# A fused vision-text layer with routed experts: two groups of short products spread among longer ones

## The chip, the cores and the metric

The kernel runs on one core of one Trainium2 chip. The metric is the device time of one execution in microseconds (us). Names used below: PE is TensorE (PEld its weight loads), DVE is VectorE, ACT is ScalarE, POOL is GpSimd, SP is SyncE.

## The reference

Images are cut into patches and embedded, joined with text tokens to 32 sequences of 165 tokens of width 192, and go through a linear attention and a softmax attention. What matters here is the end of the last layer, on all 32 x 165 = 5280 tokens:

```python
x = x + gelu(x @ mlp_w1 + mlp_b1) @ mlp_w2 + mlp_b2      # the plain layer, 192 -> 768 -> 192
xm = _ln(x, ln2_g, ln2_b)
logits = xm @ gate_w.T + gate_b                          # 4 experts
topv, topi = jax.lax.top_k(logits, 2)
gates = jax.nn.softmax(topv, axis=-1)
comb = jnp.einsum('bnk,bnke->bne', gates, onehot)
for e in range(4):
    he = gelu(xm @ exp_w1[e] + exp_b1[e])
    moe_out = moe_out + comb[..., e:e + 1] * (he @ exp_w2[e] + exp_b2[e])
return x + moe_out
```

## The kernel before

The attention part fills the first 770 us and is not touched. The plain layer works on GROUPS = 11 groups of GT = 480 tokens, each group as TG = 4 tiles of TB = 120. On every engine a function `step(n)` holds the work of group n, in an order written out by hand; semaphores alone tie the engines together. After the eleven steps come 25 turns of `turn(i)`, one for each tile of 480 rows of an expert's list, from turn -1, which only has a first layer.

PE's part of step n, in its order:

- `up(n)`: the first layer, KH = 6 blocks of five products with 480 moving columns each (operands split in a high and a low part: XH, XL, XS), alternating between banks 2 and 3. ACT takes each block with a gelu to GF and copies its high part to GH, DVE makes the low part GL.
- `tokens_in(n + 1)`: eight transposes of the next group's tokens X (in step 10 `rows_T(0)`, of expert rows RT).
- `down(n, ..., (0, 1))`: output tiles 0 and 1 of the second layer, into banks 4 and 5. A tile is KH pairs of products, one with GH (384 columns) and one with GL (192), and a bias product. In tile 0 each pair waits until its GL is there.
- `gated_T(n - 1)`: eight transposes of the normed output R of the group before; ACT scales them into ZF.
- output tile 2 (bank 6).
- `gate(n - 1, n)`: the router's logits, four tiles of two fp32 products with only 4 moving columns. The trace shows each fp32 product as two records, so one gate is 16 of them. They go to the end of bank 7.
- `prefix(n - 2, n)`: eight products of the chosen experts `sel` (16, 12, 8 and five times 4 columns), which count how many tokens before each one go to the same expert; to the end of bank 4, for the last two groups of bank 7.
- output tile 3 (bank 7).

DVE's part of step n: `mlp_sum(n - 1)` (X<-PS, twice) and the layer norm's statistics (`st`, `mv`, `ve`) among GL of blocks 0 to 3, then `x2_normed` (R<-X,mv,rs, L1294), which needs POOL's `rs` (L696), then GL of blocks 4 and 5, then the low parts of the next group's tokens (XL, XS), in steps 1 to 4 the low part of an expert's weights (w2r, 1.36 us), in step 8 `plan_early()` (L1354 to L1371), and then the router of group n - 2: `routing` (lg, top, ldf, ..., sel), `weights` (which waits for POOL's `lex`), `prefix_read` and `positions` (pos, carry, ..., dest).

POOL's part of step n: `rs` of group n - 1, the transfer of X to out, two row transfers to the experts' lists (expert_rows<-R,dest), `lex` (which needs `ldf`), two more, and four of the next group, which need `dest`.

Semaphores named by the change: `zf_ready` (ACT has made ZF), `ldiff_ready` (DVE has made ldf, the last reader of the gate's columns in bank 7), `sel_ready`, `down_read` (DVE has read the output banks), `prefix_read_done`. In turn 0 the order on PE is `up` for tile 1 with `gated_T(10)` in its middle, output tiles 0 to 2, `gate(10)`, `rows_T(2)`, `prefix(9)`, output tile 3; in turn 1 `prefix(10)` stands ahead of output tile 3. ACT's `row_high(2)` and DVE's `row_low(2)` (XL<-ZF,XH, L1249) need `rows_T(2)`, and the first layer of tile 2 needs them.

## Time and profile before

| | us |
|---|---|
| median of 3 runs (lowest, highest) | 1386.32 (1385.67, 1396.26) |
| profiled execution | 1383.22 |
| its span, first to last instruction | 1381.5 |
| PE, DVE, ACT, POOL busy in it | 1253.2, 986.9, 664.1, 423.0 |
| mean granted clock of TensorE | 0.961 |

All views below are of the one profiled execution, whose own time is 1383.22 us: 1.7 us lie outside its span. Times in the views count from the start of the span. A granted clock of 1.00 is 2.4 GHz, 0.50 is 1.2 GHz. Steps 0 to 10 begin (first product of `up`) at 771.93, 788.81, 807.08, 828.02, 847.71, 868.10, 888.46, 908.72, 928.82, 949.92 and 970.26 us, turn -1 at 989.97 us.

### The profile page before, as it was taken

What the parts mean: (1) busy time and instruction counts of PE and PEld (TensorE: products, weight loads), DVE (VectorE), ACT (ScalarE), POOL (GpSimd) and SP (SyncE); (2) the same over time, 40 slices, a digit from 0 to 9 for tenths busy, and PEclk for the clock granted to TensorE, in tenths of its full rate; (3) what the DMA queues carried; (4) which work ended last, traced back from release to release, by engine and by line L of the source; (5) the groups of instructions that cost most, each with busy time, mean ns of one, the idle gap of its engine ahead of it and who ended that gap; (6) DMA issues with size and microseconds to landing.
All of it is one profiled execution on the core that took longest, in us unless ns stands there. A gap on an engine that the chain in (4) does not pass through costs nothing.

```text
span 1381.5 us, 28231 instructions
## 1 busy us (share of the span) xinstructions
PE 1253.2 (91%) x9938; PEld 1052.7 (76%) x9938; DVE 986.9 (71%) x2685; ACT 664.1 (48%) x1520; POOL 423.0 (31%) x395
## 2 busy tenths in 40 slices
PE   4589999999999999999987899999989999999996
PEld 3377777777777777777765788898778899899995
DVE  3367777777777777777764767667778878878884
ACT  0154555545555455554555745434543444444541
POOL 1111111111011110111100037677657544544545
PEclk8689999999999999999997999999999999999998
DMA  2092211022110221102400424235466666666653
GB/s 91 21 253 52 61 52 52 15 60 60 52 52 14 60 60 52 54 13 60 97 8 9 191 46 80 62 83 147 86 183 183 151 165 165 146 178 154 148 123 33
DMA packets 93596, 123.32 MB, mean 89 GB/s; under 512 B 9152, under 2 KB 85801, under 8 KB 89554
## 3 DMA queue, kind: packets, MB, share of 16 engines
q1 hardware_dynamic: 69090, 100.75, 24.3%
q0 software_dynamic: 24432, 21.62, 10.5%
q8 instruction: 42, 0.69, 0.2%
q14 instruction: 32, 0.26, 0.1%
HBM read 68.94 MB, written 53.38 MB: 89 GB/s over the span
## 4 chain that ended last, share of the span: by engine, by line
PE 61%; DVE 19%; issue 11%; POOL 5%; ACT 3%; DMA 1%; POOLq 0%; DVEq 0%; SPq 0%; ACTq 0%
PE PS L1486 52%; PE PS L1489 9%; POOL rs L624 2%; DVE st L1010 2%; POOL expert_rows L690 2%; DVE XA L1021 1%; DVE nb L1086 1%; DVE mv L1013 1%; DVE Z L1021 1%; DVE R L1294 1%; DVE GL L1255 1%; ACT GF L925 1%; DVE H L1053 1%; ACT XAT L744 1%; POOL rs L696 1%
## 5 line engine op out<-in xcount | busy, mean ns | idle before, releaser
L1486 PE MATMUL PS<-w2r,GH 128*120 (+1 forms) x864 | 268.3, 369 | 3.1 <-DVE GL L1255 2.4
L925 ACT ACTIVATE GF<-PS,b1c 128x480 f32<-128x480 f32 x216 | 142.1, 658 | 261.0 <-PE PS L1486 248.7
L624 POOL TENSOR_TENSOR rs<-ve,minus_half 128x3 f32<-128x3 f32 (+1 forms) x80 | 58.9, 736 | 625.9 <-DVE ve L1015 625.9
L728 POOL DMA_INDIRECT out<-YO,ids x100 | 173.2, 1732 | 169.0 <-DVE flag L1439 134.3
L1486 PE MATMUL PS<-w2r,GL 128*120 (+1 forms) x864 | 221.4, 256 | 0.0
L766 ACT ACTIVATE PX<-PS,nb 128x165 f32<-128x165 f32 x576 | 176.9, 413 | 66.2 <-DVE nb L1086 57.7
L1486 PE MATMUL PS<-XH,w1r 128*128 128x480 f32 x432 | 172.3, 399 | 10.1 <-ACT GF L925 4.8
L1486 PEld LDWEIGHTS PS<-w2r,GH 128*120 128x120 f32 x864 | 161.5, 187 | 8.5 <-DVE GL L1255 8.1
L1486 PEld LDWEIGHTS PS<-w2r,GL 128*120 128x120 f32 x864 | 164.2, 190 | 0.0
L1489 PE MATMUL PS<-ident,PX 128*128 128x128 f32 x864 | 138.7, 289 | 19.7 <-DVE PT L1091 11.7
L1086 DVE TENSOR_REDUCE nb<-PS 128x6 f32<-128x990 f32 x96 | 113.5, 1184 | 50.8 <-PE PS L1486 50.4
L1489 PEld LDWEIGHTS PS<-ident,PX 128*128 128x128 f32 x864 | 95.7, 144 | 64.0 <-issue 30.0
L744 ACT ACTIVATE PT<-PS 128x384 f32<-128x384 f32 x144 | 72.6, 504 | 121.4 <-PE PS L1489 121.4
L1486 PE MATMUL PS<-XS,w1r 128*128 128x480 f32 x432 | 130.4, 383 | 0.0
L1091 DVE COPY PT<-PS 128x384 f32<-128x384 f32 x144 | 79.7, 554 | 64.2 <-PE PS L1489 63.8
L1486 PEld LDWEIGHTS PS<-XH,w1r 128*128 128x128 f32 x432 | 83.0, 192 | 43.2 <-ACT GF L925 23.0
L1486 PE MATMUL PS<-K,Q 64*128 64x165 f32 (+1 forms) x1536 | 106.3, 314 | 1.6 <-DVE K L1098 1.2
L690 POOL DMA_INDIRECT expert_rows<-R,dest x88 | 93.4, 1062 | 35.7 <-issue 24.8
L1262 DVE TENSOR_TENSOR GL<-GF,GH 128x480 fp32r<-128x480 f32 x150 | 99.3, 662 | 5.2
L1486 PEld LDWEIGHTS PS<-K,Q 64*128 64x128 f32 (+1 forms) x1536 | 80.5, 160 | 19.3 <-issue 12.1
L1486 PEld LDWEIGHTS PS<-XS,w1r 128*128 128x128 f32 x432 | 82.0, 190 | 12.6
L1486 PE MATMUL PS<-XL,w1r 128*128 128x480 f32 x216 | 82.6, 382 | 0.0
(249 smaller groups left out, 2313.1 us busy)
## 6 DMA issues: line engine op xcount, KB each, us to landing
w1r<-expert_w_parts SPq DMA_DIRECT2D x25, 1536.0 KB, 7.2
expert_rows<-empty SPq DMA_DIRECT2D x45, 369.4 KB, 5.9
RT<-expert_rows SPq DMA_DIRECT2D x25, 369.4 KB, 3.9
X<-x_scratch SPq DMA_DIRECT2D x11, 360.0 KB, 4.1
out<-X POOLq DMA_DIRECT2D x11, 360.0 KB, 5.6
XP<-in_patches SPq DMA_DIRECT2D x32, 108.0 KB
H<-in_txt SPq DMA_DIRECT2D x16, 192.0 KB, 3.8
out<-H SPq DMA_DIRECT2D x16, 192.0 KB
```

Source lines behind the costliest of these rows:

```text
L624: nc.gpsimd.tensor_tensor(rs[:, k - 1, 0:n], ve[:, k - 1, 0:n], eps_half[:, 0:n], ALU.pow).then_inc(rstd_ready[k - 1], 1)
L690: nc.gpsimd.indirect_dma_start(listd[:, :], bass.IndirectOffsetOnAxis(ap=dest[:, n % 2, t, k:k + 1], axis=0), R[n % RBUF][:, t, :], None, ...
L728: nc.gpsimd.indirect_dma_start(out[:, :], bass.IndirectOffsetOnAxis(ap=ids[:, i, t:t + 1], axis=0), YO[:, i % 2, t, :], None, bounds_check ...
L744: return nc.scalar.activation(dst, src, ACT.Copy, scale=scale)
L766: last = nc.scalar.activation(PX[:, u % 2, c, to:to + S], PS[:, 2 * (u % 2) + r, c * S:(c + 1) * S], ACT.Exp, bias=nb[:, u, 3 * r + c:3 * ...
L925: nc.scalar.activation(GF[:, m % 3, :], PS[:, 2 + m % 2, 0:GT], ACT.Gelu, bias=bias, scale=1.0).then_inc(gelu_ready, 1)
L1010: last = nc.vector.bn_stats(st[:, k - 1, t, :], src(t))
L1086: nc.vector.tensor_reduce(nb[:, u, :].rearrange("p (a s) -> p a s", a=2), src, AX_X, ALU.min).then_inc(max_ready, 1)
L1091: cp(*probT_views(g)).then_inc(probT_dve_ready, 1)
L1262: tt(GL[at][:, m, :], GF[:, m % 3, :], GH[at][:, m, :].bitcast(F32), ALU.subtract).then_inc(hid_ready, 1)
L1486: return nc.tensor.matmul(o, l, r, start=start, stop=stop)
L1489: return nc.tensor.transpose(o, x, ident[0:rows, 0:rows])
```

## The change

`gate` now makes one tile per call and `prefix` one of its shifts per call, and both are called from inside `up` and `down`. The gate of group n - 2 stands in step n behind blocks 2, 3, 4 and 5 of `up` (before: the gate of group n - 1 in step n, in one piece ahead of output tile 3). The prefix products of group n - 2 stand behind the first four pairs of output tile 3, the last five of them together behind the fourth. Ahead of output tile 3 PE waits for `ldiff_ready` of group n - 2, since the tile's bank holds the gate that DVE reads. Step 10 keeps a gate in one piece (group 9), besides that of group 8 in `up`; step 1 has none. In turn 0 the gate of group 10 goes behind the pairs of output tile 0, `rows_T(2)` behind tile 0, and the prefix of group 9 among the pairs of tile 2; in turn 1 the prefix of group 10 among those of tile 2. The products themselves and their number stay.

```diff
-        def up(s, at, w, ms):
+        def up(s, at, w, ms, gate_of=None):
...
                 mm(o, w(3, m), xs, False, True).then_inc(up_ps, 1)
+                if gate_of is not None and m >= KH - TG:
+                    gate(gate_of, s, m - KH + TG)
...
-        def down(s, gh, gl, w, bias, ts):
+        def down(s, gh, gl, w, bias, ts, prefix_of=None, gate_of=None):
...
                     mm(bank[:, 0:D], gl[:, k, TB * t:TB * t + TB], w(k, D), False, False)
+                    if prefix_of is not None and k < TG:
+                        prefix(prefix_of, s, k)
+                    if gate_of is not None and k < TG:
+                        gate(gate_of, s, k)
...
-        def gate(n, s):
-
-            pe.wait_ge(zf_ready, n + 1)
-            pe.wait_ge(down_read, s * TG + 3 + 1)
-            if n > 0:
-                pe.wait_ge(ldiff_ready, n)
-            for t in range(TG):
-                o = PS[0:TB, 7, GATE_AT + NE * t:GATE_AT + NE * t + NE]
-                for k in range(2):
-                    last = mm(o, ZF[:, k, TB * t:TB * t + TB], gwf[:, k, :], k == 0, k == 1)
-            last.then_inc(gate_ps, 1)
+        def gate(n, s, t):
+            if t == 0:
+                pe.wait_ge(zf_ready, n + 1)
+                pe.wait_ge(down_read, s * TG + 3 + 1)
+                if n > 0:
+                    pe.wait_ge(ldiff_ready, n)
+            o = PS[0:TB, 7, GATE_AT + NE * t:GATE_AT + NE * t + NE]
+            for k in range(2):
+                last = mm(o, ZF[:, k, TB * t:TB * t + TB], gwf[:, k, :], k == 0, k == 1)
+            if t == TG - 1:
+                last.then_inc(gate_ps, 1)
...
         def step(n, at):
             later = n > 0
             pe.wait_ge(actT_ready, n + 1)
-            up(n, at, mlp_w1, range(KH))
+            up(n, at, mlp_w1, range(KH), n - 2 if n > 1 else None)
...
             down(n, GH[0], GL[0], mlp_w2, b2r[:, 0, :], (2,))
-            if later:
-                gate(n - 1, n)
             if n > 1:
-                prefix(n - 2, n)
-            down(n, GH[0], GL[0], mlp_w2, b2r[:, 0, :], (3,))
+                pe.wait_ge(ldiff_ready, n - 1)
+            if n == GROUPS - 1:
+                for t in range(TG):
+                    gate(n - 1, n, t)
+            down(n, GH[0], GL[0], mlp_w2, b2r[:, 0, :], (3,), n - 2 if n > 1 else None)
...
-                down(GROUPS + i, GH[at], GL[at], w2, b2, (0, 1, 2))
-                if i == 0:
-                    gate(last, GROUPS)
+                    down(GROUPS, GH[at], GL[at], w2, b2, (0,), None, last)
                     rows_T(2)
-                if i < 2:
-                    prefix(last - 1 + i, GROUPS + i)
+                    down(GROUPS, GH[at], GL[at], w2, b2, (1,))
+                else:
+                    down(GROUPS + i, GH[at], GL[at], w2, b2, (0, 1))
                 if i == 1:
                     pe.wait_ge(ldiff_ready, GROUPS)
+                down(GROUPS + i, GH[at], GL[at], w2, b2, (2,), last - 1 + i if i < 2 else None)
```

How this moves the instructions on PE. Before, between output tiles 2 and 3 of each of the steps 2 to 10 (w2r,GH and w2r,GL are a pair of an output tile, b2r,ones its bias product, gwf,ZF the gate, sel the prefix; here a product counts once, not as two records):

```order
L1486 MATMUL PS<-b2r,ones 120x192
L1486 MATMUL PS<-gwf,ZF 120x4 [waits ldiff_ready,down_read,zf_ready]
L1486 MATMUL PS<-gwf,ZF 120x4 x7
L1486 MATMUL PS<-sel,earlier 120x16 [waits prefix_read_done,down_read,sel_ready]
L1486 MATMUL PS<-sel,ones 120x12
L1486 MATMUL PS<-sel,ones 120x8
L1486 MATMUL PS<-sel,ones 120x4 x5
L1486 MATMUL PS<-w2r,GH 120x384 [waits down_read]
```

Now, in the same place:

```order
L1486 MATMUL PS<-b2r,ones 120x192
L1486 MATMUL PS<-w2r,GH 120x384 [waits down_read,ldiff_ready]
L1486 MATMUL PS<-w2r,GL 120x192
L1486 MATMUL PS<-sel,earlier 120x16 [waits prefix_read_done,down_read,sel_ready]
L1486 MATMUL PS<-w2r,GH 120x384
L1486 MATMUL PS<-w2r,GL 120x192
L1486 MATMUL PS<-sel,ones 120x12
```

Two more pairs follow, with the 8-column product behind the first of them and the five of 4 columns behind the second. The gate has gone from here, and the wait for sel stands one pair into tile 3 instead of one gate ahead of it.

Now, on PE at the end of `up` in steps 2 to 10 (XH, XL and XS with w1r are the five products of a block, ident,X the transposes of the next group):

```order
L1486 MATMUL PS<-XS,w1r 128x480 x2
L1486 MATMUL PS<-gwf,ZF 120x4 x2
L1486 MATMUL PS<-XH,w1r 128x480 [waits gelu_ready]
L1486 MATMUL PS<-XL,w1r 128x480
L1486 MATMUL PS<-XH,w1r 128x480
L1486 MATMUL PS<-XS,w1r 128x480 x2
L1486 MATMUL PS<-gwf,ZF 120x4 x2
L1489 MATMUL PS<-ident,X 128x120 [waits x_in0]
```

Each of the last four blocks is followed by one tile of the gate; before, the blocks and the transposes followed each other directly.

## Rows read from the trace of the kernel before

**Rows 1.** The page's parts 1 and 4: busy time, chain that ended last

```profile
PE 1253.2 (91%) x9938; PEld 1052.7 (76%) x9938; DVE 986.9 (71%) x2685; ACT 664.1 (48%) x1520; POOL 423.0 (31%) x395
...
PE 61%; DVE 19%; issue 11%; POOL 5%; ACT 3%; DMA 1%; POOLq 0%; DVEq 0%; SPq 0%; ACTq 0%
```

**Rows 2.** Windows (length, PE busy, PEclk, DMA), gate to next step, ten steps

```profile
803.61:807.08 3.47, 3.47 (x32) 1.00 0.16 37
821.79:828.02 6.23, 6.23 (x39) 0.67 0.08 18
843.41:847.71 4.30, 4.30 (x39) 1.00 0.32 86
...
903.07:908.72 5.65, 5.65 (x39) 0.74 0.27 72
...
985.66:989.97 4.31, 4.31 (x40) 1.00 0.37 99
sum 52.53, PE 52.53; mean PE 5.25
```

**Rows 3.** Windows, the seven stretches at the lower clock

```profile
823.86:830.69 6.83, 6.83 (x26) 0.50 0.10 28
...
sum 27.35, PE 27.35; mean PE 3.91
```

**Rows 4.** Windows, a run of short products in turn 0

```profile
1014.24:1017.48 3.24, 3.24 (x35) 1.00 0.71 214
```

**Rows 5.** Timeline of PE in step 7 (start, length, operation, count)

```profile
923.34 1.76 PE L1486 MATMUL PS<-gwf,ZF 128*120 128x4 f32 x16
...
925.07 0.87 PE L1486 MATMUL PS<-sel,ones 120*120 120x12 f32 x7
...
927.06 0.56 PE L1486 MATMUL PS<-w2r,GH 128*120 128x384 f32 x1
```

**Rows 6.** Timeline of PEld in step 7; brackets: idle time, who ended it

```profile
913.35 0.19 PEld L1486 LDWEIGHTS PS<-XH,w1r 128*128 128x128 f32 x1 [0.25 <-ACT GF L925]
...
917.93 0.18 PEld L1486 LDWEIGHTS PS<-w2r,GH 128*120 128x120 f32 x1 [0.34 <-DVE GL L1255]
```

**Rows 7.** Windows of output tile 0, steps 2 to 10: their sum

```profile
sum 22.39, PE 20.04; mean PE 2.23
```

**Rows 8.** Windows of output tile 2 in step 6

```profile
901.22:902.96 1.74, 1.74 (x15) 1.00 0.34 65
```

**Rows 9.** Timeline of DVE in step 5

```profile
875.10 1.51 DVE L1294 TENSOR_SCALAR R<-X,mv,rs 120x192 f32<-120x192 f32 x4
...
879.49 0.17 DVE L1304 TENSOR_TENSOR ldf<-lg,top 120x16 f32<-120x16 f32 x1
```

**Rows 10.** Timeline of POOL around step 5

```profile
873.68 1.38 POOL L696 TENSOR_TENSOR rs<-ve,minus_half 120x4 f32<-120x4 f32 x1 [2.08 <-DVE ve L1286]
...
879.75 2.98 POOL L683 TENSOR_TENSOR lex<-euler,ldf 120x16 f32<-120x16 f32 x1 [0.18 <-DVE ldf L1304]
...
888.39 1.00 POOL L690 DMA_INDIRECT expert_rows<-R,dest  x1 [0.30 <-issue]
```

**Rows 11.** Timeline of DVE in step 8

```profile
940.12 0.17 DVE L1354 TENSOR_TENSOR jump<-carry,region 120x4 f32<-120x4 f32 x1
...
943.78 0.17 DVE L1304 TENSOR_TENSOR ldf<-lg,top 120x16 f32<-120x16 f32 x1
...
945.03 0.18 DVE L1313 TENSOR_SCALAR sel<-rank 120x16 fp32r<-120x16 f32 x1
```

**Rows 12.** Timeline of DVE in turns 0 and 1

```profile
1019.61 0.66 DVE L1249 TENSOR_TENSOR XL<-ZF,XH 128x480 fp32r<-128x480 f32 x1 [5.90 <-ACT XS L904]
...
1026.64 0.40 DVE L1261 CAST GH<-GF 128x480 fp32r<-128x480 f32 x1
```

**Rows 13.** Timeline of PE in turns 0 and 1

```profile
1021.04 0.45 PE L1486 MATMUL PS<-XH,w1r 128*128 128x480 f32 x1 [1.55 <-issue]
...
1028.64 0.48 PE L1486 MATMUL PS<-XH,w1r 128*128 128x480 f32 x1 [1.85 <-ACT GF L925]
```

More of the change, by code:

```diff
@@ L1829, in prefix @@
-        def prefix(n, s):
-            pe.wait_ge(sel_ready, n + 1)
-            pe.wait_ge(down_read, s * TG + 3 + 1)
-            if n > 0:
-                pe.wait_ge(prefix_read_done, n)
-            o, w = PS[0:TB, prefix_bank(n), PREFIX_AT:PREFIX_AT + TG * NE], TG * NE
-            mm(o, earlier[:, :], sel[:, :], True, False)
-            for d in range(1, TG):
-                mm(o[:, NE * d:w], ones[0:TB, :], sel[:, 0:w - NE * d], False, d == TG - 1)
-            o = PS[0:TB, prefix_bank(n), PREFIX_AT + w:PREFIX_AT + w + NE]
-            for t in range(TG):
-                last = mm(o, ones[0:TB, :], sel[:, NE * t:NE * t + NE], t == 0, t == TG - 1)
-            last.then_inc(prefix_ps, 1)
+        def gate(n, s, t):
[9 more added lines that the diff above has]
+                last.then_inc(gate_ps, 1)
@@ new lines, in prefix @@
+        def prefix(n, s, d):
+            o, w = PS[0:TB, prefix_bank(n), PREFIX_AT:PREFIX_AT + TG * NE], TG * NE
+            if d == 0:
+                pe.wait_ge(sel_ready, n + 1)
+                pe.wait_ge(down_read, s * TG + 3 + 1)
+                if n > 0:
+                    pe.wait_ge(prefix_read_done, n)
+                mm(o, earlier[:, :], sel[:, :], True, False)
+            else:
+                mm(o[:, NE * d:w], ones[0:TB, :], sel[:, 0:w - NE * d], False, d == TG - 1)
+            if d == TG - 1:
+                o = PS[0:TB, prefix_bank(n), PREFIX_AT + w:PREFIX_AT + w + NE]
+                for t in range(TG):
+                    last = mm(o, ones[0:TB, :], sel[:, NE * t:NE * t + NE], t == 0, t == TG - 1)
+                last.then_inc(prefix_ps, 1)
@@ L1868, in step @@
             down(n, GH[0], GL[0], mlp_w2, b2r[:, 0, :], (2,))
-            if later:
-                gate(n - 1, n)
             if n > 1:
-                prefix(n - 2, n)
-            down(n, GH[0], GL[0], mlp_w2, b2r[:, 0, :], (3,))
+                pe.wait_ge(ldiff_ready, n - 1)
+            if n == GROUPS - 1:
+                for t in range(TG):
+                    gate(n - 1, n, t)
+            down(n, GH[0], GL[0], mlp_w2, b2r[:, 0, :], (3,), n - 2 if n > 1 else None)
         tokens_in(0)
```

1 line of the change is left out of this document (added).

## The prediction

> **What bounds the kernel now.** I read the busy times and the chain of work that ended last first: PE is busy for 91% of the span and holds 61% of the chain [rows 1]. The change touches the eleven steps of the plain layer and two turns, about 789 to 1039 us, so the question is what PE's time there is made of. Windows over the ten steps, each from the first gate product to the first product of the next step, answer it. Steps 3 and 10 need 4.30 and 4.31 us for gate, prefix and output tile 3 with the clock granted in full. Seven others hold the same work and need 5.48 to 6.23 us at a mean granted clock of 0.67 to 0.77 [rows 2]. The clock goes to 0.50, the 1.2 GHz level, behind gate and prefix, in seven of the nine steps that have both, and stays there for 3.4 us, in step 2 for 6.8 us; 27.35 us in all [rows 3]. In step 7 the gate's 16 records take 1.76 us and seven prefix products 0.87 us, and the GH products behind them take 0.56 us each [rows 5]; at the full clock they take 0.35 us. PE was never idle there: before each fall it did 2.5 us of products with 4 to 16 columns. Gate alone (step 1) brought no fall [rows 2], nor did gate, transposes and prefix in turn 0 [rows 4].
>
> The second loss of PE in a step is waiting. In output tile 0 it waits for GL of blocks 4 and 5 (0.34 us in one row), in `up` for the gelu of two blocks before (0.25 us in one row) [rows 6]. Nine output tiles 0 take 22.39 us [rows 7], one without waits 1.74 us [rows 8]: 22.39 - 9 x 1.74 = 6.7 us. In `up`, three gaps as in rows 6 occur per step, and part of each hides behind the product before; I take 0.2 us a step, 2.1 us over nine with rounding up: 8.8 us of waits together.
>
> **Direct cost: none.** The number of products stays. A load for a short product takes about 0.105 us of PE's time (2.52 us for 24 of them in step 7, of which rows 5 show the gate's 16 with 1.76). Behind a 480-column product the first load is hidden, but then that of the next block is not, so four records cost four loads again, 0.42 us. Step 1 loses its gate (-1.66 us), step 10 has two (+1.66 us). If spreading cost or saved one load per place, it would be 0.1 us x 8 places x 9 steps = 7 us either way; I take zero, since the loads in rows 5 run at the same rate at both ends of the run.
>
> **The clock: -12.8 us.** Gate to next step in steps 2 to 10 takes 52.53 - 3.47 = 49.06 us; nine times 4.31 are 38.8, so 10.3 us are lost there [rows 2]. The stretches reach 5.0 us in all into the next steps (2.67 of them in step 3: 830.69 - 828.02), at half speed another 2.5 us. With gates between blocks of 1.09 us and prefix products between pairs of 0.28 us, the longest run of short products is five, 0.5 us, where there were 24 in 2.5 us. I expect no fall in steps 2 to 9. Bounds: nothing (the falls stay) and 27.35 / 2 = 13.7 us.
>
> **The waits: -6.6 us.** A gate tile of 0.42 us behind blocks 2 to 5 lets ACT, whose gelu and copy take 1.19 us a block against 1.09 us for PE, catch up; and 0.42 us more PE work lies between block 5 and the pairs that wait for it. DVE pays a little: x2_normed (1.51 us) stands ahead of GL 4 and 5, starting 7.0 us into step 5 and ldf 11.4 us [rows 9]. Behind the stretched blocks GL 5 ends about 0.45 us later, while PE comes to its pair about 0.9 us later. So the 8.8 us would go, but the next limit is near. DVE and POOL form a loop: x2_normed to the end of ldf 4.6 us (875.10 to 879.66), lex 3.15, six row transfers at 1.30 us each 8.0, rs 1.4 [rows 9, 10]: 17.2 us, and 18.5 where DVE makes w2r (1.36 us). PE's own work in a step is 6.54 + 1.66 + 0.75 + 4 x 1.76 + 0.75 + 0.85 = 17.6 us, against 20.1 to 20.4 us for most steps now. I leave 0.4 us each in steps 4 and 5, 0.8 in step 9 (it follows step 8, whose transfers start late) and 0.1 in the others: 2.2 us stay, 6.6 go. Bounds: 8.8 and 0.
>
> **The new waits: +1.2 us.** Ahead of output tile 3 PE now waits for ldf, and one pair later for sel; behind them in PE's queue stand tile 3 and the whole next first layer. In an ordinary step ldf is ready 11.5 us and sel 13.2 us after the start, and PE comes there after about 15.1: nothing. In step 8 plan_early (940.12 to 943.4) comes first, ldf ends 15.1 us after the step's start at 928.82 and sel 16.4 [rows 11]; both shift by 0.5. PE would wait 0.5 us for ldf and 0.9 for sel; of it 0.3 is there already, before the gate, for the same ldf. 1.2 us net; bounds 0.5 and 2.5.
>
> **Step 10: +0.5 us.** It keeps 16 gate records in a row, with a thinned prefix behind them, so a fall (about 1.5 us) stays possible; one in four. The wait ahead of gated_T in this step, for DVE's row_low, stays.
>
> **Turns 0 and 1: -2.7 us.** The first layer of tile 2 starts at 1021.04 after a gap of 1.55 us [rows 13], exactly when DVE has finished XL and XS, which began at 1019.61 after 5.90 us of waiting for ACT [rows 12], which waited for rows_T(2). Moved behind output tile 0, these transposes come 4 us earlier: the 1.7 us go. Block 5 of tile 2 then starts at 1028.64 [rows 13] because the GH that frees its buffer is made at 1026.64 [rows 12], behind row_out, weights, positions and routing of DVE. row_out of tile 3 would begin about 1.7 us earlier in step with PE, and no longer behind row_low and row_out of tile 2; that shortens 2.0 us of wait by 1.0. Bounds: 0 and 3.7.
>
> **Sum.** -12.8 - 6.6 + 1.2 + 0.5 - 2.7 = -20.4 us. Against the profiled execution: 1383.2 - 20.4 = 1362.8. The median before, 1386.3, lies 3.1 us above it, so **1366 us** is the forecast for a median. All bounds at their good ends give 1360, but not all at once; main case 1360 to 1372.
>
> **Rivals.**
>
> - *The freed time turns into waits on DVE and POOL (1374 us).* If the loop above closes at 18.6 us in all nine steps instead of 17.8, because transfers on POOL take 1.4 us now and then and rs comes late, 7 to 8 us come back. For: the loop is only 0.4 us under PE's work. Against: POOL still idles 2.08 us ahead of rs in step 5 [rows 10].
> - *The falls have another cause and stay (1378 us).* Only the waits and the turns count: -6.6 + 1.2 - 2.7 = -8. For: two steps with the same run had no fall. Against: all seven falls come behind this very run, none in a window without it between 777 and 1040 us. The Trainium skill's page "TensorE: Matmul & The Clock Gate", Part 1, ties a fall to stretches in which the PE idles; by that rule a packed run of short products would not count, and moving them would change nothing of the clock. The trace disagrees: PE has no idle time in these windows (5.65 busy of 5.65 us). The same page, Part 4, says that transposes do not count as PE work like products do; by it the last gate tile and the eight transposes now form one stretch. Turn 0, with gate, transposes and prefix in a row and the clock at 1.00, shows that such a stretch alone does no harm.
> - *Slower (1396 us).* If a mixture of short and long products counts as little work, `up` with its gates and transposes and tile 3 with its prefix would each bring a fall: up to 19 of them in place of 7 that cost as much as 8, each 12.8 / 8 = 1.6 us: +17.6, less 8 from waits and turns: +10. It turns slower from 13 falls on. Against: tiles and blocks around make up over half of any such stretch.
> - *Nothing moves (1385 us).* If PE's queue took loads ahead so that the spread makes no difference, and gains end in waits. The order on PE shows the move, so this is small.
>
> **Chances.** Main case 0.62, loop 0.20, falls stay 0.09, slower 0.04, nothing 0.05. A measurement of this kernel tells about 1% (14 us) from no change. Faster by over 1% means below 1372.5: nearly all of the main case and half of the loop case, 0.71. Slower by over 1%: 0.03. The rest, 0.26, lies within. Range: the main case reaches from 1360 to 1372; with the loop case and a part of the third it goes to 1377, and 1359 below leaves room for the median of before.
>
> **What the changed profile would show.** Granted clock 1.00 from 789 to 985 us; steps 5 to 7 at 17.7 to 18.1 us; loads of GH in output tile 0 without gaps; in step 8 a gap at w2r,GH for ldf and one at sel; step 10 about 0.7 us longer than now; the first layer of tile 2 straight behind tile 3. It is wrong if the clock still falls in the steps, or if PE's gaps name GL with rs and R late ahead of it.

## The result and the profile after

In one sitting on one chip the kernel before ran at 1387.04 us (median, 1385.67 to 1396.26) and the changed kernel at 1374.62 us (median of 4 runs, 1368.88 to 1377.07). The ratio is 0.986, 95% interval 0.9823 to 0.9897: faster by 1.4%. The quotient of those two medians is 0.991 and lies outside this interval; the record gives the ratio without its working. Two more sittings with the same kernel gave 0.9869 (0.9835 to 0.9902) and 0.9855 (0.9821 to 0.9889), and there the medians agree with them (0.9855 and 0.9852). One execution of b1 below was slow at 2957.35 us: its ratio leaves it out, its median does not. The profiled execution took 1368.88 us with a span of 1367.1, against 1383.22 and 1381.5.

The page of the changed kernel, parts 1, 2 (TensorE's granted clock) and 4, answers to [rows 1]:

```profile
PE 1236.9 (90%) x9938; PEld 1043.0 (76%) x9938; DVE 986.1 (72%) x2685; ACT 666.7 (49%) x1520; POOL 411.9 (30%) x395
...
PEclk7699999999999999999997899999999999999998
...
PE 59%; DVE 16%; issue 12%; POOL 7%; ACT 3%; another core or an unknown queue 1%; DMA 1%; POOLq 0%; DVEq 0%; SPq 0%; ACTq 0%
```

PE does the same 9938 products in 16.3 us less busy time. The shares of the chain hardly move, but for an entry that stands for updates whose sender the trace does not show; more of that below.

**Where the time went.** I measure each step from the start of its first layer to the start of the next one's, since gate and prefix no longer stand together. Windows of the changed kernel (length, busy time of PE, PEld, DVE, ACT and POOL, then granted clock, DMA share, GB/s): steps 1, 2, 6, 7, 8, 9 and 10:

```profile
787.46:804.05 16.59, 16.02 (x100) 14.14 (x99) 11.52 (x27) 9.36 (x17) 2.83 (x2) 1.00 0.40 98
804.05:821.85 17.80, 17.80 (x125) 16.89 (x123) 14.40 (x45) 9.70 (x16) 5.67 (x3) 1.00 0.28 42
...
876.99:894.78 17.79, 17.79 (x125) 16.87 (x123) 13.42 (x46) 9.69 (x16) 14.22 (x12) 1.00 0.43 85
894.78:912.60 17.82, 17.82 (x125) 16.91 (x123) 13.49 (x46) 9.57 (x16) 13.94 (x12) 1.00 0.42 85
912.60:931.76 19.16, 18.27 (x125) 16.95 (x123) 15.52 (x59) 9.68 (x16) 12.54 (x11) 1.00 0.30 55
931.76:950.71 18.95, 18.36 (x125) 16.84 (x123) 13.88 (x50) 9.56 (x16) 15.86 (x13) 1.00 0.81 230
950.71:971.07 20.36, 19.64 (x141) 18.59 (x139) 13.80 (x49) 11.21 (x18) 14.24 (x12) 1.00 0.50 114
```

All stand at clock 1.00. Steps 3, 4 and 5 take 18.36, 18.31 and 18.47 us. Steps 2 to 9 together, in one window of the kernel before and one of the changed kernel:

```profile
807.08:970.26 163.18, 160.86 (x978) 145.32 (x977) 112.96 (x380) 74.88 (x128) 106.90 (x82) 0.92 0.40 88
```

```profile
804.05:950.71 146.66, 144.91 (x979) 135.16 (x977) 113.32 (x379) 77.02 (x128) 105.67 (x80) 1.00 0.43 93
```

That is 16.5 us less for the same products. Step 1 loses 1.7 us (18.27 to 16.59), step 10 gains 0.65 (19.71 to 20.36), turns -1 and 0 lose 1.7 (31.07 to 29.39), turn 1 gains 0.5 (17.59 to 18.12). Tile 3's turn is 0.05 longer. From the start of step 1 to the start of tile 4's first layer (the "stretch" below) the length falls from 264.67 to 246.02 us: **-18.65 us**. Another 1.35 us were already there at the start of step 1, ahead of everything the change touches. From tile 5 on nothing differs (311.91 and 311.97 us to the end of the span).

**Waits of the steps.** Loads of PE in the changed kernel with the idle time ahead of them: output tile 0 of step 4, output tile 3 of step 8, output tile 0 of step 9:

```profile
850.49 0.18 PEld L1486 LDWEIGHTS PS<-w2r,GH 128*120 128x120 f32 x1 [0.25 <-DVE GL L1255]
851.06 0.18 PEld L1486 LDWEIGHTS PS<-w2r,GH 128*120 128x120 f32 x1 [0.29 <-DVE GL L1255]
...
928.08 0.18 PEld L1486 LDWEIGHTS PS<-w2r,GH 128*120 128x120 f32 x1 [0.34 <-DVE ldf L1304]
...
929.33 0.18 PEld L1486 LDWEIGHTS PS<-sel,earlier 120*120 120x120 f32 x1 [0.97 <-DVE sel L1313]
...
942.67 0.18 PEld L1486 LDWEIGHTS PS<-w2r,GH 128*120 128x120 f32 x1 [0.79 <-DVE GL L1255]
```

The gaps in `up` that [rows 6] show are gone in steps 2 to 9, and with them those of output tile 0 in steps 2, 6, 7 and 8. The two new gaps of step 8 come from DVE's timeline, where the early plan still stands ahead of the routing, as in [rows 11]:

```profile
924.20 0.16 DVE L1354 TENSOR_TENSOR jump<-carry,region 120x4 f32<-120x4 f32 x1
...
927.85 0.17 DVE L1304 TENSOR_TENSOR ldf<-lg,top 120x16 f32<-120x16 f32 x1
...
929.10 0.18 DVE L1313 TENSOR_SCALAR sel<-rank 120x16 fp32r<-120x16 f32 x1
```

**The turns.** Tile 2's first layer now starts at 1000.46, straight behind the last product of tile 3 (1000.35), where [rows 13] have a gap of 1.55 us. Loads of PE in turn 1, and DVE ahead of the second gap:

```profile
1006.98 0.19 PEld L1486 LDWEIGHTS PS<-XH,w1r 128*128 128x128 f32 x1 [1.22 <-ACT GF L925]
1018.54 0.19 PEld L1486 LDWEIGHTS PS<-XH,w1r 128*128 128x128 f32 x1 [1.56 <-issue]
```

```profile
1016.19 0.42 DVE L1436 TENSOR_SCALAR YO<-PS,cs 120x192 f32<-120x192 f32 x1 [3.02 <-PE PS L1486]
...
1017.82 0.65 DVE L1250 TENSOR_TENSOR XS<-ZF,XS 64x480 fp32r<-64x480 f32 x1
```

The gap of 1.56 us is new: tile 3's first layer waits for XS (ends 1018.47), which DVE makes behind `row_out` of output tiles 0 and 1. DVE stood idle for 3.02 us in front of the second `row_out`, although PE's last product of output tile 1 was long issued:

```profile
1012.46 0.26 PE L1486 MATMUL PS<-b2r,ones 128*120 x1
```

The signal of that tile is recorded only at 1016.16, 3.4 us behind the modelled end of this product; in an undisturbed trace such a signal follows within 0.02 us. So the gap doesn't come from the order of DVE's work. It is the first effect of a disturbance that costs more in tile 4's turn.

**A wait that no part of the change explains.** Tile 4's turn takes 21.70 us instead of 16.08. A load of PE, ACT's gelu and DVE's `row_out` there:

```profile
1041.42 0.29 PEld L1486 LDWEIGHTS PS<-XH,w1r 128*128 128x128 f32 x1 [5.99 <-ACT GF L925]
```

```profile
1040.70 0.66 ACT L925 ACTIVATE GF<-PS,b1c 128x480 f32<-128x480 f32 x1 [11.47 <-remote]
```

```profile
1037.74 0.42 DVE L1436 TENSOR_SCALAR YO<-PS,cs 120x192 f32<-120x192 f32 x1 [3.88 <-remote]
```

By the profile, PE's products that ACT and DVE wait for ended long before: the first two blocks ran from 1033.48 to 1035.84, tile 3's last product started at 1033.37. The signals are recorded at 1037.71 for DVE and 1040.57 for ACT, 4.1 and 5.8 us behind. The ends of PE's products are modelled, so the trace can't tell whether the signals or the products themselves were late; "late signal" below means either. PE then stood idle, and the only lower-clock stretch behind step 0 and before the end of the span follows:

```profile
1040.93:1044.34 3.41, 2.92 (x7) 2.48 (x8) 2.96 (x10) 1.51 (x3) 3.10 (x2) 0.50 0.56 56
```

So against the profiled execution of before: -1.35 - 18.65 + 5.6 = -14.4 us. The experiments have two questions: which part of the -18.65 comes from what, and whose are the 5.6 us.

A comparison of the kept traces helps with the second. Of PE's 1154 signals, 21 to 39 come over 0.3 us late or have no record in the changed kernel's trace and in a1 to a4 and c1 to c3; in before, b1 to b4 and d1 it is none or one. Each of the steps 2 to 9 of the changed kernel is within 0.3 us of the same step in b1, so it costs little there. In turn 1 all eight disturbed traces have DVE waits for PE of 1.3 to 3.0 us and the six others have none, b2 with its prefix spread in the same way included.

### The profile page after: what moved, and what is told of

It reads as the page before. It is cut to its first block, busy times and chain, and to the rows that moved or that the text cites. A ratio compares the mean times of both kernels' runs of the same rounds, so it can differ in the third digit from the quotient of the medians.

```text
span 1367.1 us, 28240 instructions
## 1 busy us (share of the span) xinstructions
PE 1236.9 (90%) x9938; PEld 1043.0 (76%) x9938; DVE 986.1 (72%) x2685; ACT 666.7 (49%) x1520; POOL 411.9 (30%) x395
## 4 chain that ended last, share of the span: by engine, by line
PE 59%; DVE 16%; issue 12%; POOL 7%; ACT 3%; another core or an unknown queue 1%; DMA 1%; POOLq 0%; DVEq 0%; SPq 0%; ACTq 0%
PE PS L1486 51%; PE PS L1489 8%; POOL expert_rows L690 3%; POOL rs L624 2%; DVE st L1010 2%; DVE XA L1021 1%; DVE nb L1086 1%; DVE mv L1013 1%; DVE Z L1021 1%; DVE H L1053 1%; ACT XAT L744 1%; POOL out L678 1%; DVE ZS L1068 1%; DVE H L1050 1%
## 5 line engine op out<-in xcount | busy, mean ns | idle before, releaser
L1486 PE MATMUL PS<-w2r,GH 128*120 (+1 forms) x864 | 262.8, 362 | 1.7 <-DVE GL L1255 1.1
L728 POOL DMA_INDIRECT out<-YO,ids x100 | 163.0, 1630 | 184.2 <-DVE flag L1439 158.1
L1486 PE MATMUL PS<-w2r,GL 128*120 (+1 forms) x864 | 216.9, 251 | 0.0
L1486 PEld LDWEIGHTS PS<-w2r,GH 128*120 128x120 f32 x864 | 156.9, 182 | 4.9 <-DVE GL L1255 4.2
L1486 PEld LDWEIGHTS PS<-w2r,GL 128*120 128x120 f32 x864 | 159.1, 184 | 0.0
```

The costliest lines, as they stand in the source:

```text
L728: nc.gpsimd.indirect_dma_start(out[:, :], bass.IndirectOffsetOnAxis(ap=ids[:, i, t:t + 1], axis=0), YO[:, i % 2, t, :], None, bounds_check ...
L1486: return nc.tensor.matmul(o, l, r, start=start, stop=stop)
```

## The experiments

Each kernel was timed in several runs beside the kernel before on the same chip. There were four sittings, each on another chip: a1 to a4, b1 to b4, c1 to c3, d1. The stretch is that of the profiled execution. In the diffs - and + are against the changed kernel, unless another is named.

| kernel | median us | before us | ratio (95%) | steps 1 to 10 | stretch | tile 4's turn |
|---|---|---|---|---|---|---|
| before | | | | 201.16 | 264.67 | 16.08 |
| a1_again | 1368.47 | 1388.60 | 0.9869 (0.9835, 0.9902) | 183.74 | 246.37 | 22.08 |
| a2_gates_spread_only | 1376.72 | 1388.60 | 0.9901 (0.9872, 0.9929) | 187.17 | 249.90 | 22.28 |
| a3_prefix_spread_only | 1388.37 | 1388.60 | 1.0005 (0.9978, 1.0032) | 195.73 | 258.06 | 21.85 |
| a4_turns_only | 1390.64 | 1388.60 | 1.000 (0.9974, 1.0026) | 200.37 | 262.67 | 22.87 |
| b1_steps_only | 1367.25 | 1380.57 | 0.9892 (0.9862, 0.9922) | 183.27 | 246.60 | 15.72 |
| b2_rows_back | 1365.19 | 1380.57 | 0.9892 (0.9862, 0.9922) | 183.41 | 247.77 | 16.08 |
| b3_plan_later | 1369.75 | 1380.57 | 0.9924 (0.9896, 0.9953) | 181.07 | 244.57 | 16.07 |
| b4_gate_behind_up | 1370.30 | 1380.57 | 0.9906 (0.9880, 0.9932) | 185.40 | 249.57 | 16.06 |
| c1_scatter_held | 1370.85 | 1393.56 | 0.9847 (0.9816, 0.9878) | 183.68 | 245.98 | 20.48 |
| c2_load_held | 1376.32 | 1393.56 | 0.9888 (0.9854, 0.9921) | 183.70 | 250.33 | 22.78 |
| c3_as_changed | 1372.91 | 1393.56 | 0.9855 (0.9821, 0.9889) | 183.67 | 246.34 | 21.58 |
| d1_rows_behind_tile1 | 1366.41 | 1387.67 | 0.9847 (0.9812, 0.9883) | 181.67 | 244.17 | 15.72 |

### The changed kernel again, and its parts alone

**a1_again** is the changed kernel unchanged.

> The changed kernel itself once more. Its first profile shows the steps and turns 0 and 1 some 18.6 us shorter than before, as forecast, but then one gap of 6 us (PE waiting for ACT in the first layer of tile 4, with DVE and ACT idle behind late PE signals), which gives 5.6 us back; and its unprofiled runs (1373 to 1377 us) lie above the profiled one (1368.9). Theory A: the gap belongs to the new order (the turns now meet the POOL transfers at another time), then this profile shows it again at the same place, 5 to 6 us. Theory B: it is an accident of that execution, then it is absent or elsewhere and the profiled time is about 1363 us plus or minus 3. Either way the ratio to before should be 0.983 to 0.990.

The wait of tile 4 came again (5.28 us at 1039.86), so it is no accident of one execution.

**a2_gates_spread_only**: gates behind the blocks, prefix in one piece ahead of output tile 3.

```
             if n > 1:
+                for d in range(TG):
+                    prefix(n - 2, n, d)
-            down(n, GH[0], GL[0], mlp_w2, b2r[:, 0, :], (3,), n - 2 if n > 1 else None)
+            down(n, GH[0], GL[0], mlp_w2, b2r[:, 0, :], (3,))
```

> As the changed kernel, but in steps 2 to 10 the eight prefix products stand in one piece ahead of output tile 3 (turns as in the changed kernel). If the clock falls because of the run of 24 short products, then 8 in a row (0.85 us) bring no fall and the time is that of the changed kernel within 2 us. If every short run in that place is enough, falls come back in up to 9 steps and cost 1.6 us each, up to +14 us. The wait for sel in step 8 grows by 0.3 us.

Windows of steps 7 and 8, and the lower-clock stretch in step 8:

```profile
898.23:916.06 17.83, 17.83 (x124) 16.92 (x123) 13.47 (x45) 9.69 (x16) 14.30 (x12) 1.00 0.42 85
916.06:938.40 22.34, 20.40 (x124) 19.24 (x123) 15.72 (x62) 9.44 (x16) 14.78 (x13) 0.89 0.27 53
933.60:940.40 6.80, 6.80 (x26) 6.49 (x27) 3.03 (x11) 0.00 (x0) 5.66 (x5) 0.50 0.15 42
```

An ordinary step is as long as in the changed kernel (17.83 against 17.82): spreading the prefix saves nothing there. Step 8 takes 3.2 us more: PE waits 1.87 us in one piece for sel, up to 933.46, and the clock falls at 933.60, as the packed prefix begins. Here the wait is what stands ahead of the fall; in steps 6 and 7 the same packed prefix without a wait brought none.

**a3_prefix_spread_only**: prefix between the pairs, gate (of the group one later) in one piece ahead of output tile 3.

```
-            up(n, at, mlp_w1, range(KH), n - 2 if n > 1 else None)
+            up(n, at, mlp_w1, range(KH))
...
-            if n > 1:
-                pe.wait_ge(ldiff_ready, n - 1)
-            if n == GROUPS - 1:
+            if later:
                 for t in range(TG):
                     gate(n - 1, n, t)
```

> As the changed kernel, but in the steps the gate of group n - 1 stands in one piece ahead of output tile 3, as before; the prefix stays among the pairs (turns as in the changed kernel). No work now fills PE's waits in up and in output tile 0: by the forecast's terms 6.6 us come back, and no wait for ldf in step 8 beyond that of before (-0.9). The clock: 16 short products and then a thinned prefix; if only the whole packed run makes it fall, it stays at 1.00 (changed kernel +6 us, 1380); if gate and thinned prefix are enough in some steps, +1.5 us for each, up to +13 more.

**a4_turns_only**: the steps in the order of before, turns 0 and 1 as changed.

```
-            up(n, at, mlp_w1, range(KH), n - 2 if n > 1 else None)
+            up(n, at, mlp_w1, range(KH))
...
-            if n > 1:
-                pe.wait_ge(ldiff_ready, n - 1)
-            if n == GROUPS - 1:
+            if later:
                 for t in range(TG):
                     gate(n - 1, n, t)
-            down(n, GH[0], GL[0], mlp_w2, b2r[:, 0, :], (3,), n - 2 if n > 1 else None)
+            if n > 1:
+                for d in range(TG):
+                    prefix(n - 2, n, d)
+            down(n, GH[0], GL[0], mlp_w2, b2r[:, 0, :], (3,))
```

> The steps as before (gate and prefix in one piece ahead of output tile 3), only turns 0 and 1 as in the changed kernel. The forecast's term: 2.7 us faster than before (1384), with the 1.7 us gap ahead of the first layer of tile 2 gone and the seven falls kept. If the new order of the turns is what brings the 6 us gap in tile 4, the profile shows that gap here too and the time is 3 us above before.

Here step 7 can be taken apart. Its window in a4 (gate and prefix in one run, clock falls), and in a3 (gate in one run, prefix spread, no fall in this step):

```profile
910.61:931.01 20.40, 20.10 (x125) 18.19 (x123) 13.30 (x45) 9.34 (x16) 14.26 (x12) 0.92 0.36 74
```

```profile
907.06:926.24 19.18, 18.54 (x124) 16.66 (x123) 13.33 (x46) 9.33 (x16) 14.02 (x11) 1.00 0.40 79
```

In this step a fall costs 1.2 us, not 1.6: the slower PE waits less. The gaps ahead of its loads, added up from the timeline, are 1.42 us in a4 and 1.76 in a3; the difference lies in output tile 0 (0.50 against 0.84). The a3 timeline of PEld shows what stays at the full clock, five gaps; these are the first three and the largest:

```profile
910.27 0.19 PEld L1486 LDWEIGHTS PS<-XH,w1r 128*128 128x128 f32 x1 [0.16 <-ACT GF L925]
911.46 0.19 PEld L1486 LDWEIGHTS PS<-XH,w1r 128*128 128x128 f32 x1 [0.24 <-ACT GF L925]
912.64 0.19 PEld L1486 LDWEIGHTS PS<-XH,w1r 128*128 128x128 f32 x1 [0.24 <-ACT GF L925]
916.52 0.18 PEld L1486 LDWEIGHTS PS<-w2r,GH 128*120 128x120 f32 x1 [0.84 <-DVE GL L1255]
```

With only the prefix thinned out the clock still fell twice in ten steps (886.38 for 3.4 us, 944.41 for 6.8) instead of seven times. So 16 gate records with a thin prefix behind them are sometimes enough.

The timed runs don't agree with the trace of a3: its stretch is 6.6 us shorter than that of before, its ratio 1.0005 (0.9978 to 1.0032), and 1380 us had been expected, or 1383 with its two falls, against a median of 1388. Where the difference went is open. The turns alone measure as nothing: 1.000.

### Apart, but not spread

**b1_steps_only** takes the changed steps with turns 0 and 1 in the order of before.

```
-                    down(GROUPS, GH[at], GL[at], w2, b2, (0,), None, last)
-                    rows_T(2)
-                    down(GROUPS, GH[at], GL[at], w2, b2, (1,))
-                else:
-                    down(GROUPS + i, GH[at], GL[at], w2, b2, (0, 1))
+                down(GROUPS + i, GH[at], GL[at], w2, b2, (0, 1, 2))
+                if i == 0:
+                    for t in range(TG):
+                        gate(last, GROUPS, t)
+                    rows_T(2)
+                if i < 2:
+                    for d in range(TG):
+                        prefix(last - 1 + i, GROUPS + i, d)
...
-                down(GROUPS + i, GH[at], GL[at], w2, b2, (2,), last - 1 + i if i < 2 else None)
```

> The eleven steps as in the changed kernel, turns 0 and 1 in the order of before (gate of group 10 in one piece behind three output tiles, then the row transposes, then the prefix; in turn 1 the prefix ahead of output tile 3). Theory A (the new order of the turns makes the stretch of late semaphore updates and the 6 us wait ahead of tile 4's output): steps at 17.8 to 18.4 us, tile 4 back at about 16 us, median 1362 to 1365, ratio 0.982. Theory B (the stretch comes because everything stands some 18 us earlier against the transfers, whatever the order of the turns): tile 4 takes about 22 us again, median 1369 to 1371.

**b2_rows_back** is the changed kernel with only `rows_T(2)` back behind output tile 2.

```
                     down(GROUPS, GH[at], GL[at], w2, b2, (0,), None, last)
-                    rows_T(2)
...
                 down(GROUPS + i, GH[at], GL[at], w2, b2, (2,), last - 1 + i if i < 2 else None)
+                if i == 0:
+                    rows_T(2)
```

> The changed kernel with one group of row transposes of turn 0 (tile 2's) back behind output tile 2; gate tiles and prefix spread as in the changed kernel. If the early row transposes, which start the load and scatter of later tiles sooner, make the stall of tile 4: tile 4 back at about 16 us, the first layer of tile 2 again 1.5 us late, median about 1364. If the gate products in output tile 0 and the earlier routing make it: tile 4 stays at 22 us, median 1370.

In turn 0 of b1 gate, row transposes and prefix stand in one run again, as in before. There [rows 4] the clock stayed; here it fell 0.3 us behind the run:

```profile
997.96:1001.20 3.24, 3.24 (x35) 3.24 (x33) 0.00 (x0) 0.57 (x1) 2.71 (x2) 1.00 0.68 203
1001.49:1004.90 3.41, 3.22 (x14) 3.00 (x13) 1.49 (x4) 1.81 (x3) 0.00 (x0) 0.50 0.25 27
```

The same run brought a fall in b3 (996.25) and b4 (1009.06, 6.8 us), and PE had no gap in the 8 us ahead of any of the three. One execution in which a packed run kept the clock does not show it harmless.

Windows of tile 4's turn in b1 and in b2:

```profile
1037.09:1052.81 15.72, 14.87 (x92) 13.29 (x91) 14.23 (x46) 6.63 (x10) 11.76 (x9) 1.00 0.70 184
```

```profile
1034.11:1050.19 16.08, 14.88 (x93) 13.29 (x91) 15.02 (x46) 6.52 (x10) 11.52 (x9) 1.00 0.72 186
```

Without the early row transposes tile 4 is back at 16 us in both, and the traces alone would have closed the case: `rows_T(2)` makes the stall. The timings do not agree, and b1's median of 1367 us missed the 1362 to 1365 expected. By the traces b1 should lie 5 us below the changed kernel against the same before, by its ratio it lies level or above (0.9892 against 0.9855 to 0.9869). These two were on another chip than the a kernels; see "Whose are the 5.6 us".

**b3_plan_later** is b1 with DVE's early plan behind the routing.

```
-            if n - 3 == EARLY_GROUPS - 1:
-                plan_early()
             if n > 1:
                 routing(n - 2)
+            if n - 3 == EARLY_GROUPS - 1:
+                plan_early()
+            if n > 1:
                 weights(n - 2)
```

> As the steps-only kernel, and in step 8 DVE makes the early plan behind the routing instead of ahead of it. The waits of step 8 for ldf and sel (0.34 and 0.97 us in the changed kernel) should go and step 8 come to 18.0 us: 1.2 us less than the steps-only kernel, if the 3.3 us of the plan do not come late for the weights; in that case step 9 gets longer by up to 1 us and the sum stays.

Windows of its steps 7 and 8:

```profile
894.47:912.29 17.82, 17.82 (x125) 16.92 (x123) 13.45 (x46) 9.70 (x16) 14.04 (x12) 1.00 0.42 85
912.29:930.07 17.78, 17.78 (x125) 16.87 (x123) 15.85 (x62) 9.69 (x16) 14.05 (x12) 1.00 0.34 65
```

Step 8 loses both waits (19.17 to 17.78) and step 9, whose gap of 0.79 us was its echo, falls from 18.96 to 18.00: 2.35 us for a move of one line. The timed runs did not show it (0.9924 against 0.9892 for b1, overlapping intervals); five of the six ran at a mean clock of 0.962 to 0.966 and the profiled one at 0.972.

**b4_gate_behind_up** is b1 with nothing spread: the gate's 16 records in one piece behind `up`, the prefix in one piece ahead of output tile 3.

```
-            up(n, at, mlp_w1, range(KH), n - 2 if n > 1 else None)
+            up(n, at, mlp_w1, range(KH))
+            if n > 1:
+                for t in range(TG):
+                    gate(n - 2, n, t)
...
+            if n > 1:
+                for d in range(TG):
+                    prefix(n - 2, n, d)
-            down(n, GH[0], GL[0], mlp_w2, b2r[:, 0, :], (3,), n - 2 if n > 1 else None)
+            down(n, GH[0], GL[0], mlp_w2, b2r[:, 0, :], (3,))
```

> As the steps-only kernel, but the gate's 16 records stand in one piece behind the first layer and the prefix in one piece ahead of output tile 3: nothing is spread, the two are only apart. If the fall of the clock needs gate and prefix in one run (24 short products), none comes and the steps take 18.0 to 18.8 us (only the waits inside the first layer, 0.2 us a step, stay): 1 to 4 us above the steps-only kernel. If every packed run of 16 short products brings one, seven to nine falls come back at 1.6 us each: 11 to 15 us above it.

Window of its step 7:

```profile
902.51:920.53 18.02, 18.02 (x124) 16.66 (x123) 13.45 (x45) 9.45 (x16) 14.29 (x12) 1.00 0.41 84
```

This is the experiment that says most of the mechanism. No fall in steps 2 to 9, and they take 147.35 us against 146.37 in b1. (Step 10, which keeps a gate directly ahead of the prefix, had one.) So two runs, of 16 and of 8 short products, three output tiles apart, kept the clock in all eight steps, where one run of 24 lost it in seven of nine. The moved gate also fills the waits of output tile 0 in b4, but missing waits are not what keeps the clock: the packed runs in turn 0 of b1, b3 and b4 had none ahead of them and the clock fell.

The fine spread is worth 1.0 us over eight steps. PE's timeline from the start of `up` to the first transpose of the next group in step 7 shows what it does, in b4 and in the changed kernel:

```profile
902.51 0.41 PE L1486 MATMUL PS<-XH,w1r 128*128 128x480 f32 x1
...
909.30 1.74 PE L1486 MATMUL PS<-gwf,ZF 128*120 128x4 f32 x16
910.91 1.02 PE L1489 MATMUL PS<-ident,X 120*128 120x120 f32 x8
```

```profile
894.78 0.40 PE L1486 MATMUL PS<-XH,w1r 128*128 128x480 f32 x1
...
902.96 1.02 PE L1489 MATMUL PS<-ident,X 120*128 120x120 f32 x8
```

Six blocks without a wait take 6 x 1.09 = 6.54 us. b4 needs 6.79 us for them and 1.61 for the packed gate, 8.40 in all; the changed kernel 8.18 for both. So the waits in `up` cost b4 0.25 us, and the gate costs 1.6 us packed or spread, 0.4 for four records. The three gaps ahead of the loads in b4's `up` (0.16, 0.23, 0.23 us) add up to 0.62, but most of that hides behind the product before: gaps of PEld are not PE's lost time. Gate ahead of the output layer also closes the gaps of output tile 0 in steps 2, 6, 7 and 8, spread or not.

### Whose are the 5.6 us

On the evidence of a and b I took it that the early row transposes pull POOL's transfers forward. In all a kernels and the changed one the row transfers of group 9 start 4.2 us behind the start of tile 2's first layer, and in the b kernels and before 6.0 us. Those of group 10 start beside the load of w1 instead of 2.7 us behind it. Two kernels were to test that collision, beside the changed kernel on one chip.

**c1_scatter_held** (changed kernel):

```
+        pool.wait_ge(down_ps, (GROUPS + 2) * TG + 2)
         scatter(GROUPS - 1)
```

> The changed kernel with one wait added on POOL: the row transfers of group 10 start only when output tile 1 of expert tile 2 stands, about 3 us later (1029.9 instead of 1026.25) and so 3 us behind the load of w1 at 1026.7 instead of just ahead of it. If the two colliding make the late semaphore updates, the 6 us wait in front of tile 4's second pair of blocks goes and tile 4 takes 16.1 us: median 5 to 6 us under the changed kernel (about 1363). If the stretch has another cause, tile 4 stays at 22 us and the time does not move or grows by up to 1 us.

**c2_load_held** (b2, with the load of w1 held):

```
             sp.wait_ge(up_ps, (GROUPS + i - 1) * KH)
+            if i == 5:
+                sp.wait_ge(down_ps, (GROUPS + 2) * TG + 2)
             load_w1(i, i % 2)
```

> The kernel with the row transposes back (no stall, tile 4 16.1 us), and the load of w1 behind expert tile 3's first layer held until output tile 1 of tile 2 stands: 1030.6 instead of 1027.2, so 0.6 us behind the start of group 10's row transfers instead of 2.7 us ahead. Tile 5, which needs it, starts at 1050. If the collision makes the stall, it comes now: tile 4 takes about 22 us, median 1370. If not, tile 4 stays at 16.1 us and the median at that of the row-transposes-back kernel, 1364 to 1365.

**c3_as_changed**:

> The changed kernel unchanged, for a comparison on the same chip. Both theories: tile 4 at 22 us, 1368 to 1374 us; against the kernel with the row transfers held it is 5 to 6 us slower if the collision is the cause, equal if not.

In c1 the transfers started at 1031.46, 4.4 us behind the load instead of 0.3 ahead of it, and ACT still waited; POOL's first transfer and ACT's gelu:

```profile
1031.46 1.05 POOL L690 DMA_INDIRECT expert_rows<-R,dest  x1 [5.04 <-PE PS L1487]
```

```profile
1042.97 0.66 ACT L926 ACTIVATE GF<-PS,b1c 128x480 f32<-128x480 f32 x1 [3.63 <-remote]
```

Tile 4's turn fell from 21.58 (c3) to 20.48 us, not to 16. The collision theory falls as I had put it. The delay moved, though: counted from the start of step 1 the transfers came 4.4 us later than in c3, and the longest late signal, of 4.2 us, belongs to a product that ends 3 to 4 us later. In c2 the stall came, with the order of b2, which had none in the sitting before:

```profile
1046.28 0.29 PEld L1488 LDWEIGHTS PS<-XH,w1r 128*128 128x128 f32 x1 [5.93 <-ACT GF L927]
```

c2 alone can't say whether the held load or the chip did it: its group 10 transfers had started at 1031.16, the load only at 1036.10. But the list of stalls now reads by sitting: all seven kernels on the chips of a and c, and the first profile of the changed kernel, have it; none of the five on the chips of b and d has it, nor the profile of before. The traces alone can't decide between chip and order, since no kernel was profiled on chips of both kinds: all six traces without the stall start the transfers of group 10 2.7 us behind the load of w1, and none of the eight with it does.

The runs of the kernel before, whose order of turns never varied, say more. Its runs at a mean granted clock of 0.965 by sitting:

```
sitting a   1386.39  1386.47
sitting b   1378.99  1379.04
sitting c   1385.96
sitting d   1379.13  1379.64
```

At the same clock the unchanged kernel is about 7 us slower on the chips where the others stall, the size of the stall (4.4 to 6.8 us in tile 4's turn and some 1.5 in turn 1). A straight line through all 56 of its runs, time against clock with one slope for the four sittings, puts a and c 6 to 8.5 us above b and d. The ratios give a second test. If only the new kernel stalled, its ratio would be worse by the stall. For a4 that is 1.0040 (6.8 us lost by tile 4, 1.3 gained by the turns) against 0.999 if both stall, and 1.000 with an upper end of 1.0026 was measured. In a1, a2, c1, c2 and c3 the interval excludes the first reading too: a1, for one, should lie at 0.9911 or at 0.9868, and measured 0.9869 (0.9835 to 0.9902). Only a3 goes the other way: 0.9994 or 0.9952, measured 1.0005 (0.9978 to 1.0032).

So **the stall most likely belongs to the chip and hits the kernel before as well**; the profile shown of before came from an execution without it. It was not seen in a trace of before, so this stays an inference. Nor does the chip explain everything: in sittings a, b and c single runs are 6 to 11 us longer than others of the same kernel at the same clock (c2 1380.87 against 1372.06 at 0.971, b3 1377.25 against 1369.29 at 0.966), and none of these was profiled. What delays the signals is open.

### A version with what was learned

**d1_rows_behind_tile1** is b3 with the gate of group 10 and `rows_T(2)` behind output tile 1 of turn 0.

```
-                down(GROUPS + i, GH[at], GL[at], w2, b2, (0, 1, 2))
+                down(GROUPS + i, GH[at], GL[at], w2, b2, (0, 1))
                 if i == 0:
                     for t in range(TG):
                         gate(last, GROUPS, t)
                     rows_T(2)
+                down(GROUPS + i, GH[at], GL[at], w2, b2, (2,))
```

> The steps of the plan-later kernel (new order of the steps, early plan behind the routing), and in turn 0 the gate in one piece and tile 2's row transposes behind output tile 1 instead of behind output tile 2; prefix between tiles 2 and 3 as before. The transposes come 1.8 us earlier than in the plan-later kernel, 4 us later than in the changed kernel. The first layer of tile 2 then starts without its 0.5 us wait and up to 1 us of the 2.1 us wait behind it goes. If the stall of tile 4 depends on how far the early transposes pull POOL's chain of transfers ahead of the load of w1, this half step decides: with the scatter of group 10 starting still at least 1.5 us behind the load, tile 4 stays at 16.1 us and the profiled span comes to 1357 to 1359 us, the best of all; with the scatter's start within 1 us of the load, the stall comes and the span is 1363 to 1365.

Windows of its steps 8 and 10, turns -1 and 0, and tile 4's turn:

```profile
919.33:937.12 17.79, 17.79 (x125) 16.88 (x123) 15.87 (x62) 9.68 (x16) 14.03 (x12) 1.00 0.34 65
954.94:976.02 21.08, 20.43 (x141) 19.38 (x139) 14.05 (x50) 11.33 (x18) 14.09 (x12) 0.96 0.47 101
976.02:1006.16 30.14, 27.21 (x162) 23.39 (x161) 23.54 (x66) 14.43 (x22) 17.27 (x13) 0.97 0.61 161
```

```profile
1038.52:1054.24 15.72, 14.87 (x92) 13.29 (x91) 14.23 (x46) 6.63 (x10) 11.76 (x9) 1.00 0.71 184
```

The stretch is the shortest of all, 244.17 us, though the clock fell once in it, at 974.33, in the thin prefix behind the gate of step 10. The span of 1366.1 us missed the 1357 to 1359 expected: its mean clock was 0.964, and step 1 began 7 us later than in b3. Turns -1 to 1 take 47.66 us, against 48.63 in b3 and 47.51 in the changed kernel. The ratio is 0.9847 (0.9812 to 0.9883). By the stretch it is 1.9 us better than the changed kernel, which the timings can't confirm.

## Why the prediction was right

The forecast was 1366 us and the median came to 1374.62: inside the stated range to 1377, but outside the main case of 1360 to 1372, and next to the 1374 of a rival whose mechanism did not occur. Against the profiled execution the forecast was -20.4 us, and the stretch that the change touches lost 18.65: -17.55 in steps 1 to 10 (forecast -12.8 - 6.6 + 1.2 + 0.5 = -17.7) and -1.1 in the turns (forecast -2.7). The profiled execution took 1368.88 us where 1383.2 - 20.4 = 1362.8 was forecast. Of the 6.1 us between, late signals make 5.6 in tile 4's turn and by my estimate 1.6 in turn 1, which nothing in the prediction knew of; 1.35 come back from ahead of step 1, which the change doesn't touch and which is luck. The median lies 5.7 us above the profiled execution, where the forecast took 3.1. By its terms:

- **Clock, forecast -12.8.** The falls went, all seven, and steps 2 to 9 stood at 1.00. In step 7 a fall costs 1.2 us (a4 against a3), of which PE's extra work is 1.56 (20.40 - 1.42 = 18.98 against 19.18 - 1.76 = 17.42) less 0.34 of waits that a slow PE doesn't meet. The 27.0 us at the lower clock in these steps are 7.9 such stretches of 3.4: 12.3 us of PE's work. The size was right. The cause was nearly right: the fine spread was not needed, parting gate from prefix was enough (b4). One argument failed: turn 0, which "shows that such a stretch alone does no harm", had kept its clock by luck, as b1, b3 and b4 show.
- **Direct cost, forecast 0, bounds 7 either way.** Right. Four gate records took 0.4 us between blocks and 0.4 packed (8.18 us for `up` and gate against 6.54 + 1.6), and the prefix costs the same between pairs or packed (a2 17.83, changed 17.82). PE's own work in a step is 17.8 us both ways, 0.2 more than the forecast's 17.6.
- **Waits, forecast -6.6, with +1.2 for step 8.** In steps 2 to 9 of before, `up` loses 0.24 us a step at the full clock (6.78 against 6.54; forecast 0.2), output tiles 0 and 1 take 5.9 us more than eight times 3.64, and step 8 waits 0.3 for ldf: 8.2 us. The changed kernel has none in `up`, 2.8 in output tile 0 and 1.4 elsewhere, mostly the two of step 8: 4.2 us. Net -4.0, and -0.8 in step 10, against -5.4 forecast. What stays stands where it was said: about 0.5 in steps 4 and 5 and 1.1 in step 9, but also 0.5 in step 3.
- **The steps together.** For steps 2 to 9, -12.3 - 4.0 = -16.3, measured -16.5. Step 1, which loses its gate (forecast -1.66), lost 1.7.
- **Step 10.** The +0.5 was a surcharge for a possible fall, one in four; none came here. The whole step grew by 0.65 us, where the signs said 0.7. A fall behind its 16 gate records with a thin prefix was seen in step 10 of d1 (in none of the other eight traces with this step 10), and twice in the ten steps of a3, which have this order.
- **Turns, forecast -2.7.** Measured -1.1 (-1.7, +0.5 and +0.05 in tile 3). Both mechanisms came: tile 2 starts straight behind tile 3, and the wait of block 5 fell from 2.26 to 1.22 us. The gap of 1.56 us ahead of tile 3's first layer ate the second gain, and it hangs on a signal 3.4 us late. Without it tile 3 could have started at 1017.0 instead of 1018.57, which makes -2.7. That is an estimate: no trace has the order of the changed kernel without late signals.

In the prediction's loop of DVE and POOL, six transfers at 1.30 us are 7.8 and not 8.0, and its rival names 17.8 for what was added up to 17.2; neither changes the sum.

The rivals: the DVE and POOL loop did not close; steps 6 and 7 have no gap at all, and only in steps 3 to 5 do 0.5 us remain. The rival with falls of another cause rested on the rule of the Trainium skill's page "TensorE: Matmul & The Clock Gate", Part 1. The runs speak against it for these falls: PE had no idle time from the gate to the fall [rows 2] in six of the seven and 0.3 us in step 8, and in b4, which has the same products in the same steps and only parts the two runs, they are gone. Other falls do come behind waits: that of a2's step 8 behind 1.87 us of idle PE, those of a1 and c3 in turn 0 (980.15 and 984.76) behind two waits of 1.1 us, and that of tile 4 while PE had stood still for five us; there the trace goes with the rule. The slower rival, mixed stretches that count as little work, is ruled out by the spread steps at 1.00. The signs I had named all came but one: clock 1.00, steps 6 and 7 at 17.8 (step 5 at 18.47), the two gaps of step 8, step 10, tile 2 straight behind tile 3. The clock of 1.00 up to 985 us held in this execution and not in a1 and c3.

## What to carry to other kernels

Where the clock falls behind one long run of small products, it is enough to break the run at a place where the first half has its inputs early; a finer spread mainly fills waits. Measure a wait by when the next product starts, not by the idle time of the weight loads: 0.62 us of such gaps was 0.25 us of time. A packed run that kept the clock in one profile can lose it in the next. And a wait that two traces show differently is the change's only if both were taken on the same chip: nine traces seemed to show a cause here, until c2 stalled with the order that had been free of it and the equal-clock times of the unchanged kernel pointed to the chip.

## What the hardware showed that I had not expected

- In eight traces of fourteen, at the same places of the program each time, signals of PE reached DVE and ACT up to 4 and 6 us late ("remote" waits of 3.88 and 11.47 us in the changed kernel), and on the chips of seven of them the unchanged kernel was about 7 us slower at an equal mean clock.
- A stretch of 3.4 us at half the clock cost a PE-bound step 1.2 us, not 1.7, because PE waited less behind it.
- Four gate records between two blocks of 480-column products took 0.4 us more time, the same as in a packed run.
